# A gated cross-attention and feed-forward block on one core: a reordered attention phase, with x2 of sequence three made by ACT and GpSimd

## The reference, cut to what matters

```python
q = ctx @ Wq.T + bq;  k = ctx @ Wk.T + bk              # per sequence, 256 x 128
attention = softmax(q @ k.T, axis=-1)                  # 256 x 256
x = x + tanh(g_xattn) * einsum('bln,bmn->blm', layernorm(x), attention)
h = layernorm(x).astype(e4m3)
gate, up = h @ w_gating[0], h @ w_gating[1]            # 1024 hidden, 8-bit operands
x = x + tanh(g_ffn) * ((gelu(gate) * up).astype(e4m3) @ w_linear)
```

## Time and profile before

| | us |
|---|---|
| median of 3 runs | 49.53 (49.53 to 49.55) |
| the profiled execution | 49.46 |
| its span | 47.7 |

### The profile page before, as it was taken

One profiled execution on the slowest core, in us unless ns is written; L12 is line 12 of the kernel. 1 busy time (PEld: TensorE's weight loads), 2 busy tenths in 40 slices (PEclk: granted clock), 3 DMA queues, 4 the chain that ended last, 5 costly groups with the idle time before them and its releaser, 6 DMA issues.

```text
span 47.7 us, 831 instructions
## 1 busy us (share of the span) xinstructions
PE 41.9 (88%) x242; PEld 28.4 (60%) x242; DVE 34.5 (72%) x108; ACT 29.4 (62%) x66; POOL 17.0 (36%) x35
## 2 busy tenths in 40 slices
PE   3999999963999999998999999999999999999000
PEld 1327888824788888772436555756565588863000
DVE  0103639999797979799999990987666999589700
ACT  0642937399897899655699749765555874563000
POOL 3200799039999550600700250000000599002300
PEclk9999999999999999999999999999999999999999
DMA  0499899999999970000000000000000015330092
GB/s 0 61 361 335 308 368 401 340 189 136 89 103 105 105 73 1 0 0 21 0 0 0 0 0 0 0 0 7 0 0 0 0 54 173 112 115 0 0 340 101
DMA packets 3604, 4.64 MB, mean 97 GB/s; under 512 B 400, under 2 KB 2320, under 8 KB 3600
## 3 DMA queue, kind: packets, MB, share of 16 engines
q1 hardware_dynamic: 2448, 3.61, 22.0%
q0 software_dynamic: 864, 0.79, 18.1%
q10 hardware_dynamic: 288, 0.20, 1.3%
HBM read 5.90 MB, written 1.05 MB: 146 GB/s over the span
## 4 chain that ended last, share of the span: by engine, by line
PE 63%; DVE 12%; DMA 10%; SPq 3%; issue 2%; ACT 2%; DVEq 1%
PE bank L640 14%; PE bank L600 14%; PE bank L646 14%; PE bank L665 13%; DMA x_sb<-x 10%; DVE st L415 4%; PE bank L572 4%; DVE nmax L422 2%; PE bank L622 2%; PE bank L565 2%; SPq L209 2%; DVE mv L418 1%; DVE attn L433 1%; ACT xq L349 1%; DVE yo L488 1%
## 5 line engine op out<-in xcount | busy, mean ns | idle before, releaser
L473 DVE SCALAR_TENSOR_TENSOR ap<-bank,gl 128x512 f16<-128x512 f32 (+1 forms) x19 | 11.5, 603 | 3.8 <-PE bank L646 2.2
L358 ACT ACTIVATE gl<-bank 128x512 bf16<-128x512 f32 (+1 forms) x19 | 9.8, 525 | 5.6 <-PE bank L640 5.5
L640 PE MATMUL bank<-xq,wg 128*128 128x512 fp8e4 (+1 forms) x38 | 10.0, 346 | 0.2 <-ACT xq L349 0.2
L646 PE MATMUL bank<-xq,wg 128*128 128x512 fp8e4 (+1 forms) x38 | 10.0, 346 | 0.0
L665 PE MATMUL bank<-wl,aq 128*128 128x256 fp8e4 x64 | 9.7, 273 | 0.1
L665 PEld LDWEIGHTS bank<-wl,aq 128*128 128x128 f16 x64 | 6.1, 98 | 3.5 <-DVE aq L482 0.6
L600 PE MATMUL bank<-attnT,xT_sb 128*128 128x256 f32 x32 | 8.1, 385 | 0.0
L278 POOL TENSOR_TENSOR yo<-ys,x 128x256 f32<-128x256 f32 x4 | 3.0, 776 | 9.3 <-ACT ys L366 9.3
L263 POOL TENSOR_TENSOR r<-ve,neg_half 128x2 f32<-128x2 f32 x4 | 3.0, 759 | 8.5 <-DVE ve L456 8.5
L600 PEld LDWEIGHTS bank<-attnT,xT_sb 128*128 128x128 f32 x32 | 5.6, 190 | 0.7 <-ACT attnT L332 0.2
L482 DVE TENSOR_SCALAR aq<-ap 128x512 uint16<-128x512 uint16 (+1 forms) x19 | 5.7, 302 | 0.0
(11 more groups left out here) (50 smaller groups left out, 54.7 us busy)
## 6 DMA issues: line engine op xcount, KB each, us to landing
x_sb<-x SPq DMA_DIRECT2D x4, 256.0 KB, 4.7
xT_sb<-xT SPq DMA_DIRECT2D x4, 256.0 KB, 5.9
out<-yo SPq DMA_DIRECT2D x6, 128.0 KB, 2.1
wg<-w_gating POOLq DMA_DIRECT2D x4, 128.0 KB, 8.7
par<-params_ctxT SPq DMA_DIRECT2D x1, 256.0 KB, 4.4
wl<-w_linear POOLq DMA_DIRECT2D x2, 128.0 KB, 8.7
out<-yo SPq DMA_DIRECT2D x1, 256.0 KB, 2.0
par<-params_ctxT SPq DMA_DIRECT2D x1, 192.0 KB, 2.7
```

Of the source, the lines that this page charges most:

```text
L358: nc.scalar.activation(gl[:, s % 2, toks], gate_b[s % 2][:, toks], ACT.Gelu_apprx_tanh).then_inc(gelu_ready, 1)
L473: nc.vector.scalar_tensor_tensor(ap[:, s % NAP, toks], up_b[s % 2][:, toks], ACT_SCALE, gl[:, s % 2, toks], ALU.mult, ALU.mult).then_inc(p ...
L640: mm = nc.tensor.matmul(gate_b[s % 2][:, toks], wg8[:, c, k, 0, o:o + P], xq[:, g, k, toks], start=(k == 0), stop=(k == KC - 1))
L646: mm = nc.tensor.matmul(up_b[s % 2][:, toks], wg8[:, c, k, 1, o:o + P], xq[:, g, k, toks], start=(k == 0), stop=(k == KC - 1))
```

## The change

ACT's `k_out` goes to DVE. All four `normalise` go to POOL. DVE's front queue is written anew: `k_out`, row maxima and inverted sums come between single `stats1`. `energy(1)` comes ahead of the projections of sequence 2. `scales1` is done in two halves, for two sequences each. `turn_attention` and `turn_x2` wait for one tile at a time. `shift_x` is gone: x2 is now x + s1 * (attend's result), without the shift by the mean, which a second layernorm doesn't see; the shift is added at the outputs (as a bias in `scale_out`, and by a new `shift_x2` on ACT for three tiles). `norm2(0)` moves from DVE to ACT. For sequence 3, x2 isn't made by DVE: ACT scales the PSUM bank (`scale_attention`, one tile behind each of the first two GELUs), and POOL adds x (`add_attention(t)`, behind `rstd2(1)` and the new `shifts1`). The first block of group 0 is cut by sequence too, so S = 20 and the first step needs only sequence 0. `X_AFTER` is (5, 7); ACT makes `norm2(2)` behind GELU 4 and `norm2(3)` behind GELU 6. DVE's `moments2(2)` stays behind product 2 and round 1, and `moments2(3)` comes behind product 5 and round 4 (before: product 2 and round 1).

The diff, cut to its core (left margins are narrowed; declarations are left out, and so are long runs of removed lines after their first):

```diff
     HOLD = 2
+    FIRST = 1
-    STEPS = [divmod(n, HT) + (0, GB) for n in range(G * HT - SPLIT)]
+    STEPS = [(0, j, i, i + 1) for i in range(GB) for j in range(FIRST)]
+    STEPS += [divmod(n, HT) + (0, GB) for n in range(FIRST, G * HT - SPLIT)]
     STEPS += [(G - 1, j, i, i + 1) for i in range(GB) for j in range(HT - SPLIT, HT)]
     S = len(STEPS)
-    X_AFTER = (3, 6)
+    X_AFTER = (5, 7)
+    ACT_NORM = (0, 2, 3)
...
+        first_of_g1 = next(s for s, step in enumerate(STEPS) if step[0] == 1)
         def last_step(b):
...
-    def shift_x(b):
+    def scales1(h):
-        pool.wait_ge(nms1_ready, 1)
...
+        pair = slice(h * B // 2, (h + 1) * B // 2)
+        pool.wait_ge(mv1_ready, LT * (h + 1) * B // 2)
+        nc.gpsimd.tensor_scalar(ve1[:, pair], mv1[:, pair, :, 1], EPS, None, ALU.add).then_inc(ve1_ready, 1)
+        pool.wait_ge(ve1_ready, h + 1)
+        nc.gpsimd.tensor_tensor(r1[:, pair], ve1[:, pair], neg_half[:, pair], ALU.pow).then_inc(r1_ready, 1)
+        pool.wait_ge(r1_ready, h + 1)
+        if h == 0:
+            pool.wait_ge(ntg_ready, 1)
+        nc.gpsimd.tensor_scalar(s1[:, pair], r1[:, pair], tg[:, 0:1], None, ALU.mult).then_inc(s1_ready, 1)
-    def scales1():
+    def shifts1():
-        pool.wait_ge(mv1_ready, LT * B)
...
         nc.gpsimd.tensor_scalar(nr1[:, :, :], r1[:, :, :], ntg[:, 0:1], None, ALU.mult).then_inc(nr1_ready, 1)
-        nc.gpsimd.tensor_scalar(s1[:, :, :], r1[:, :, :], tg[:, 0:1], None, ALU.mult).then_inc(s1_ready, 1)
         pool.wait_ge(nr1_ready, 1)
...
+    def add_attention(t):
+        pool.wait_ge(sp3_ready, t + 1)
+        nc.gpsimd.tensor_tensor(x2[:, B - 1, t], sp3[:, t], x_sb[:, B - 1, t],
+                                ALU.add).then_inc(pool_x2_ready, 1)
     def add_residual(k):
         b, t = divmod(k, LT)
-        pool.wait_ge(scaled_ready, b + 1)
+        pool.wait_ge(scaled_ready, k + 1)
         nc.gpsimd.tensor_tensor(yo[:, b, t], ys[:, b, t], x2[:, b, t], ALU.add).then_inc(pool_y_ready, 1)
...
     pool.wait_ge(consts_ready, 1)
-    scales1()
...
+    normalise(0)
+    normalise(1)
+    scales1(0)
+    normalise(2)
+    normalise(3)
+    scales1(1)
     for b in range(B):
         rstd2(b)
+        if b == 1:
+            shifts1()
+            add_attention(0)
+            add_attention(1)
     for k in range(LT * GB):
...
     pool.wait_ge(aq_ready, S)
-    pool.wait_ge(scaled_ready, GB + 1)
+    pool.wait_ge(scaled_ready, LT * GB + 1)
     nc.gpsimd.tensor_tensor(yo[:, 2, 1], ys[:, 2, 1], x2[:, 2, 1], ALU.add).then_inc(pool_y_ready, 1)
...
-    def k_out(b):
...
     def exps(b):
...
-    def shift_x(b):
...
+    def scale_attention(t):
+        if t == 0:
+            act.wait_ge(pv_done, B)
+            act.wait_ge(s1_ready, 2)
+        nc.scalar.activation(sp3[:, t], halves(pv_b[(B - 1) % 2])[:, t], ACT.Copy,
+                             scale=s1[:, B - 1, t:t + 1]).then_inc(sp3_ready, 1)
+    def shift_x2(n):
+        b, t = ((2, 0), (3, 0), (3, 1))[n]
+        if n == 0:
+            act.wait_ge(nms1_ready, 1)
+        if b < B - 1:
+            act.wait_ge(x2_ready, LT * b + t + 1)
+        else:
+            act.wait_ge(pool_x2_ready, t + 1)
+        nc.scalar.activation(x2s[:, n], x2[:, b, t], ACT.Identity,
+                             bias=nms1[:, b, t:t + 1]).then_inc(x2s_ready, 1)
     def norm2(b):
-        act.wait_ge(nmr2_ready, b - 1)
+        act.wait_ge(nmr2_ready, ACT_NORM.index(b) + 1)
         for t in range(LT):
...
-    def scale_out(b):
+    def scale_out(b, t):
         g, i = divmod(b, GB)
         act.wait_ge(ffn2_done, last_step(b) + 1)
-        if b == 0:
+        if (b, t) == (0, 0):
             act.wait_ge(yscale_ready, 1)
-        nc.scalar.activation(ys[:, b].rearrange("p t d -> p (t d)"), y_b[g][i][:, :], ACT.Copy,
+        nc.scalar.activation(ys[:, b, t], halves(y_b[g][i])[:, t], ACT.Identity, bias=nms1[:, b, t:t + 1],
                              scale=yscale[:, 0:1]).then_inc(scaled_ready, 1)
...
     q_out(0)
-    k_out(0)
     q_out(1)
-    k_out(1)
-    q_out(2)
-    k_out(2)
     exps(0)
-    q_out(3)
-    k_out(3)
+    q_out(2)
     exps(1)
+    q_out(3)
     attn_out(0)
     exps(2)
-    exps(3)
     attn_out(1)
+    exps(3)
     attn_out(2)
...
     nc.scalar.activation(table[:, :], tg[:, 0:1], ACT.Gelu_apprx_tanh)
-    shift_x(2)
     attn_out(3)
-    shift_x(3)
+    norm2(0)
     xq_out(0)
...
         gelu(s)
-        if s == X_AFTER[0] - 2:
+        if s < LT:
+            scale_attention(s)
+        if s == X_AFTER[0] - 1:
             norm2(2)
-        if s == X_AFTER[1] - 2:
+        if s == X_AFTER[1] - 1:
             norm2(3)
...
             xq_out(3)
-        if s == HT + LAG:
...
+        if X_AFTER[1] < s <= X_AFTER[1] + LT + 1:
+            shift_x2(s - X_AFTER[1] - 1)
+        if s == first_of_g1 + LAG:
+            scale_out(0, 0)
+            scale_out(0, 1)
+        if s == first_of_g1 + LAG + 1:
+            scale_out(1, 0)
+            scale_out(1, 1)
+    scale_out(2, 1)
...
         def _(dve):
-    def stats1(b):
...
+    def stats1(b, t):
+        if t == 0:
+            dve.wait_ge(s_x[b], 16)
+        nc.vector.bn_stats(st1[:, b, t], x_sb[:, b, t]).then_inc(st1_ready, 1)
+    def moments1(b):
         for t in range(LT):
...
+    def k_out(b):
+        dve.wait_ge(k_done, b + 1)
+        nc.vector.tensor_scalar(kT[:, b * L:(b + 1) * L], k_b[b % 2][:, 0:L], bk, None,
+                                ALU.add).then_inc(k_ready, 1)
     def row_max(b):
...
-    def normalise(b):
...
     def add_attention(b):
         dve.wait_ge(pv_done, b + 1)
-        dve.wait_ge(s1_ready, 1)
...
+        dve.wait_ge(s1_ready, 1 if b < B // 2 else 2)
         for t in range(LT):
-            nc.vector.scalar_tensor_tensor(x2[:, b, t], halves(pv_b[b % 2])[:, t], s1[:, b, t:t + 1], xs[:, b, t],
-                                           ALU.mult, ALU.add).then_inc(x2_ready, 1)
+            nc.vector.scalar_tensor_tensor(x2[:, b, t], halves(pv_b[b % 2])[:, t], s1[:, b, t:t + 1],
+                                           x_sb[:, b, t], ALU.mult, ALU.add).then_inc(x2_ready, 1)
     def stats2(b, t):
-        dve.wait_ge(x2_ready, LT * b + t + 1)
+        if b < B - 1:
+            dve.wait_ge(x2_ready, LT * b + t + 1)
+        else:
+            dve.wait_ge(pool_x2_ready, t + 1)
         nc.vector.bn_stats(st2[:, b, t], x2[:, b, t]).then_inc(st2_ready, 1)
...
-    def finish(b, t):
+    def finish(n):
+        b, t = ((2, 0), (3, 0), (3, 1))[n]
         g, i = divmod(b, GB)
         dve.wait_ge(ffn2_done, last_step(b) + 1)
+        dve.wait_ge(x2s_ready, n + 1)
         nc.vector.scalar_tensor_tensor(yo[:, b, t], halves(y_b[g][i])[:, t], yscale[:, 0:1],
-                                       x2[:, b, t], ALU.mult, ALU.add).then_inc(y_ready, 1)
+                                       x2s[:, n], ALU.mult, ALU.add).then_inc(y_ready, 1)
...
     nc.vector.tensor_scalar(yscale[:, :], tg[:, 1:2], 1.0 / ACT_SCALE, None, ALU.mult).then_inc(yscale_ready, 1)
-    for b in range(B - 1):
-        stats1(b)
+    k_out(0)
+    stats1(0, 0)
+    stats1(0, 1)
+    moments1(0)
+    k_out(1)
     row_max(0)
-    stats1(B - 1)
     row_max(1)
-    normalise(0)
+    invert_sum(0)
+    k_out(2)
+    stats1(1, 0)
+    k_out(3)
+    invert_sum(1)
+    stats1(1, 1)
+    moments1(1)
     row_max(2)
-    normalise(1)
+    stats1(2, 0)
     row_max(3)
-    normalise(2)
...
+    invert_sum(2)
+    stats1(2, 1)
+    moments1(2)
+    stats1(3, 0)
+    stats1(3, 1)
+    invert_sum(3)
+    moments1(3)
+    add_attention(0)
+    stats2(0, 0)
+    stats2(0, 1)
+    moments2(0)
+    add_attention(1)
+    stats2(1, 0)
+    stats2(1, 1)
+    moments2(1)
     add_attention(2)
+    norm2(1)
     stats2(2, 0)
-    stats2(2, 1)
-    moments2(2)
-    add_attention(3)
     dve.wait_ge(yscale_ready, 1)
...
             round_product(s - 1)
-        if s == 1:
-            stats2(B - 1, 0)
-            stats2(B - 1, 1)
+        if s == 0:
+            stats2(2, 1)
         if s == 2:
-            moments2(B - 1)
+            moments2(2)
+        if s == 3:
+            stats2(3, 0)
+        if s == 4:
+            stats2(3, 1)
+        if s == 5:
+            moments2(3)
     round_product(S - 1)
-    dve.wait_ge(scaled_ready, GB + 1)
...
+    dve.wait_ge(scaled_ready, LT * GB + 1)
+    finish(0)
+    finish(1)
+    finish(2)
...
-    def turn(to, src):
...
     def turn_attention(b):
...
             pe.wait_ge(ident_ready, 1)
-        if b < B - 1:
...
         if b >= 2:
...
             pe.wait_ge(q_ready, B)
-        turn(turn_b[b % 2], attn[:, b]).then_inc(attn_turned, 1)
+        for t in range(LT):
+            pe.wait_ge(pool_attn_ready, LT * b + t + 1)
+            for k in range(KC):
+                mm = nc.tensor.transpose(halves(turn_b[b % 2])[:, k, t * P:(t + 1) * P],
+                                         attn[:, b, t, k * P:(k + 1) * P], ident[:, :])
+        mm.then_inc(attn_turned, 1)
...
```

(81 more changed lines are left out.)

52 lines of the change are left out of this document (8 added, 44 removed).

## The result

The changed kernel took 51.39 us (median of 4 runs, 51.02 to 51.55) against 49.53 (4 runs, 49.49 to 49.55): a ratio of 1.037, interval 1.031 to 1.042. The forecast was 49.65, range 49.15 to 50.3: the sign was right, the size wrong by 1.7 us. The forecast gave "slower" a chance of 0.48 only, so a right sign is in part luck. The profiled execution took 51.55 with a span of 49.5.

The account below looks back on a forecast made before the run. PE's work was taken as the bound, so only holes count: 1.9 removed, 2.1 added. The end 0.12 later on the profiled 49.46 gave 49.58, plus 0.07 to the median 49.65 us; range 49.15 to 50.3.

Parts of the forecast that it names:

- The front: PE's work up to the first feed-forward matmul, forecast to start at 20.52 instead of 22.12: 1.6 gained.
- The hole that I counted as pure gain: PE's wait of 1.33 ahead of the first transposes of attention weights, forecast to close with 0.7 to spare.
- g0: Start of the first `ffn1`, the first feed-forward matmul; forecast at 20.52, against 22.12 in the kernel before.
- The hole at `energy(1)`: New PE wait for DVE's move of k of sequence 1, forecast at 0.25, 0.05 at the low end.
- The chain: Serial GELUs, products, moments and norms feeding `turn_x2(2)` and `turn_x2(3)`; forecast to end at 30.54, 0.12 later than before.
- Product 2 follows 0.64 later: Link in the feed-forward part: DVE's product 2 was to start 0.64 behind GELU 2, at 22.89.
- The tail stays: Last products, `finish` and transfers the same, ACT's `scale_out` halves and `shift_x2` fitting into PE's steps: no cost.
- Outside the span: Profiled execution's time less its span, carried over unchanged from the kernel before, at 1.76.
- Rival 2: POOL's queue, with all roots and weights, becomes the bound, by lock or slow powers: 49.9 to 50.4, chance 0.21.
- the rule against the change: POOL's sum for sequence 3 could block DVE's round 0 through shared ports: 0.3 on the chain, 49.95.
- Rivals 3 and 4: Third: chain 0.2 to 0.4 earlier, 49.15 to 49.43, chance 0.20; fourth: transposes not late, 47.9, chance 0.07.
- two holes ahead of `turn_x2(2)` and `turn_x2(3)`: PE waits for ACT's norms of sequences 2 and 3 in the feed-forward part, forecast at 0.5 and 1.2.

Follow-up runs that it names:

- a2: The kernel before with five warm-up matmuls instead of six: 49.80 us, ratio 1.011 to the kernel before.
- b2: The changed kernel with the moments of sequence 2 ahead of product 0 and those of sequence 3 behind product 4: 49.31 us, ratio 0.981 to the kernel before.
- a0: The changed kernel run again without an edit: 50.91 us, ratio 1.030 to the kernel before.
- b1: The changed kernel with POOL's second sum for sequence 3 waiting until product 2 is done: 51.57 us, ratio 1.039 to the kernel before.
- c0: The changed kernel with eight tiny memsets of an unused tile at the head of DVE's queue: 50.60 us, ratio 1.024 to the kernel before.
- b0: The changed kernel with x2 of sequence 3 made by DVE, without ACT's scalings and POOL's sums: 50.43 us, ratio 1.014 to the kernel before.
- a1: The changed kernel with seven warm-up matmuls instead of six: 50.85 us, ratio 1.029 to the kernel before.
- a3: The changed kernel with both statistics of sequence 3 behind product 3 and its moments behind product 4: 49.99 us, no ratio.
- c2: b2 with the four halves of `scale_out` one a step instead of in pairs: 49.13 us, ratio 0.987 to the kernel before.
- b3: The changed kernel with the edits of b0 and b2 together: 49.03 us, ratio 0.988 to the kernel before.
- c1: The changed kernel with five warm-up matmuls instead of six: 51.58 us, ratio 1.040 to the kernel before.

## Why the prediction was wrong

By its steps, in the profiled execution: 49.58 forecast, 51.55 measured, 1.97 to explain (the terms below add up to it but for rounding).

- **The front: +0.89.** This is the step that failed first. The layout begins with `k0` at 4.45 and `energy(0)` at 5.76, as one execution of the kernel before had them, and I took them as given for the changed kernel. They hang on when PE's full rate begins, which was 4.47 there and 6.26 here, so `energy(0)` came 0.98 late. The line on the granted clock that I opened with could not show it: the trace has no clock record ahead of full rate, and the page draws that stretch as full. The hole that I counted as pure gain would have hidden this (a2); in its price I should have asked what else it absorbs. Against b2, whose full rate began as in the kernel before and whose g0 was 20.79, the late rate cost 0.62; the other 0.27 are the layout's own.
- **The hole at `energy(1)`.** I had 0.25. It was 0.29 to 0.34 in a0, b1, b2 and c0, and 0.15 in b0, but 0.09 or less with an early full rate (a1, a3, c2) and where the late rate had held `energy(0)` back longest (the first profile, b3). DVE's move of k took 0.45 to 0.49, as priced. The distance from the first weight transposes to g0 was right: I had 10.17, the trace has 10.19.
- **The chain: +0.56.** The step that failed is "Product 2 follows 0.64 later": it followed 1.14 behind GELU 2, and 0.42 of that is the delay which c0 took away. The rest of the chain, of some 20 links laid end to end, was right to 0.14 in 10. The claim that this chain eats the gain is shown: a3 and b2 took it apart and gained 1.3 and 2.0 behind g0.
- **"The tail stays": +0.26.** It did not; the step put the term at nothing. `scale_out` was priced as fitting into PE's steps, but two halves with a bias take ACT 1.04 (whole, without it, it took 0.68 before), the next GELU is late, and POOL's sums, in turn later, hold the rounds (0.73). A hole of 0.20; c2 halves it.
- **Outside the span: +0.27.** 2.06 instead of 1.79 (my 1.76 came of rounded spans); the prediction carried the term over unchanged. b0 and b3 show that it goes with making x2 of sequence 3 on ACT and POOL, and leave open how.
- **Rival 2** (POOL) was not the cause. Its power of four took 1.04, my estimate 1.05, and `turn_x2(0)` did not wait. Round 0 did meet the second sum: both started at 23.3, the round kept its 0.22, and the sum took 0.81 instead of 0.73. So the rule against the change cost the chain nothing there. **Rivals 3 and 4** fell, since the transposes were late, as laid out.

The sum, then: ahead of g0 the kernel gained 0.72 instead of 1.6, and behind g0 it lost 2.81 instead of 1.72. The mechanism forecast (two holes ahead of `turn_x2(2)` and `turn_x2(3)` that eat the gain of the front) was right; the start of full rate, product 2, the tail and the time outside the span were what it had wrong.

## What to carry to other kernels

A hole on the bounding engine isn't only loss: it takes up whatever varies ahead of it, and a change that closes it exposes that, so price the front over its bad case too. When work is brought forward, move the whole serial chain that feeds the next meeting point, statistics and roots included; here the moments of two sequences, moved by a few steps (b2), turned a kernel 3 to 4% slower than the one before into one 1 to 2% faster. Work handed from a busy engine to two idle ones isn't free even where each has room: here it cost 0.27 outside the span and, by argument, 0.15 in the chain.

## What the runs showed of the hardware

- PE's rate at the start had the two levels that its matmuls of 256 f32 columns show (0.43 and 0.22 us each, which are 1.2 and 2.4 GHz). With six warm-ups full rate began anywhere from 3.43 (c2) to 6.26 us (the first profile of the changed kernel); with five it came later still, at 7.17 (a2) and 9.55 (c1). The clock line of the page reads full in these slices none the less, since the trace has no record there: the matmuls' spacing has to be read. The Trainium skill, page "TensorE: Matmul & The Clock Gate", section "Part 1: The HAM clock gate (the "warmup" mystery)", says that the point of transition varies because what the gate goes by does not start with the kernel. These runs show such a spread, wider than its half microsecond either way; they don't show its reason.
- An instruction of DVE can start 0.4 us behind all its semaphores depending on its place in the program, and eight tiny instructions ahead of it take the delay away (c0).
- An addition on 128x2 values in SBUF waited 0.4 us for a sum on POOL (b1), while a product with one operand in PSUM kept its 0.69 beside such a sum (c0: product at 23.44, sum until 23.78).
